# Deformable convolution band pipeline: offset bias carried by constant rows, f16 parts taken from PSUM, columns first in the offset convolution, one PSUM bank for turned windows and four for samples

## What is computed

```python
x = x + conv0(groupnorm(x))   # pair_repr @ Wa + ba, @ Wb + bb, sigmoid(@ Wg + bg),
                              # einsum('bijk,bikl->bijl', a, b), (g * ab) @ Wo + bo
x = x + conv1(groupnorm(x))   # deformable 3 x 3 convolution, below

def conv1(x, w_off, b_off, w_def):
    x = relu(x)
    offset = conv3x3(x, w_off) + b_off            # 18 values for each output pixel
    py = base_y + offset[:, :, 0]                 # 9 taps, each with a row and a column
    px = base_x + offset[:, :, 1]
    samp = bilinear_gather(x, py, px)             # 128 channels x 9 taps x pixels
    return einsum("bckhw,ock->bohw", samp, w_def)
```

## Time and profile before

| | before |
|---|---|
| median of 3 runs | 1659.01 us (1657.56 to 1660.0) |
| profiled execution, its own time | 1660.34 us |
| its span (first to last instruction) | 1658.2 us |
| PE busy | 1566.1 us, 94% |
| DVE busy | 1183.6 us, 71% |
| ACT busy | 1033.9 us, 62% |
| POOL busy | 919.9 us, 55% |

### The profile page before, as it was taken

How to read it: one execution, slowest core, us unless ns; L and a number is a source line. 1 busy time by engine, 2 the same in 40 slices (tenths; PEclk the granted TensorE clock), 3 DMA queues, 4 the chain that set the end, 5 groups by cost and what they waited for, 6 DMA issues and landing times.

```text
span 1658.2 us, 27065 instructions
## 1 busy us (share of the span) xinstructions
PE 1566.1 (94%) x8915; PEld 987.9 (60%) x8916; DVE 1183.6 (71%) x2218; ACT 1033.9 (62%) x1820; POOL 919.9 (55%) x555
## 2 busy tenths in 40 slices
PE   5999999948999999999999999999999999999998
PEld 3778787714555555555555555555555555555554
DVE  5888888745667777776777767777766777767764
ACT  2555555535666666666666666666666666666663
POOL 3555555616555555555555555555555555555561
PEclk9999999958999999999999999999999999999999
DMA  5333333245766666666666666666666666665550
GB/s 145 99 117 117 117 114 114 76 149 167 213 186 180 177 177 177 176 180 179 180 180 183 184 177 176 193 177 184 183 186 180 178 184 182 181 181 171 166 153 26
DMA packets 190601, 268.03 MB, mean 162 GB/s; under 512 B 19710, under 2 KB 128279, under 8 KB 190487
## 3 DMA queue, kind: packets, MB, share of 16 engines
q1 hardware_dynamic: 190486, 266.60, 55.0%
HBM read 188.33 MB, written 78.18 MB: 161 GB/s over the span
## 4 chain that ended last, share of the span: by engine, by line
PE 72%; issue 11%; POOL 6%; DVE 4%; SPq 3%; ACT 3%; DMA 1%; POOLq 0%; DVEq 0%; ACTq 0%
PE bank L827 29%; PE pair L796 22%; PE pair L873 9%; POOL samples_hi L1567 4%; PE pair L845 4%; PE bank L845 3%; DVE samples_lo L1359 2%; ACT samples_hi L1048 2%; PE pair L809 2%; PE pair L811 2%; POOL rstd L1542 1%; POOL samples_lo L1554 1%; SPq L490 0%; POOL weights L1619 0%; PE bank L704 0%
## 5 line engine op out<-in xcount | busy, mean ns | idle before, releaser
L1619 POOL TENSOR_TENSOR weights<-hy_all,hx_all 112x768 f32<-112x768 f32 x384 | 736.8, 1955 | 550.2 <-PE bank L827 507.0
L1359 DVE SCALAR_TENSOR_TENSOR samples_lo<-bank,samples_hi 128x288 f16<-128x288 f32 (+1 forms) x1024 | 450.7, 463 | 287.0 <-ACT samples_hi L1048 281.4
L827 PE MATMUL bank<-weights,zT 112*128 112x288 f32 (+1 forms) x2176 | 616.8, 408 | 24.2 <-DVE samples_lo L1359 24.0
L1048 ACT ACTIVATE samples_hi<-bank 128x288 f16<-128x288 f32 (+1 forms) x1024 | 413.6, 418 | 360.7 <-PE bank L827 330.3
L827 PEld LDWEIGHTS bank<-weights,zT 112*128 112x128 f32 x2176 | 374.5, 190 | 186.7 <-DVE samples_lo L1359 74.0
L796 PE MATMUL pair<-samples_hi,w_hi 128*128 128x512 f16 x576 | 218.8, 380 | 1.3 <-DVE samples_lo L1359 1.3
L796 PE MATMUL pair<-samples_lo,w_hi 128*128 128x512 f16 x576 | 217.5, 378 | 0.0
L796 PE MATMUL pair<-samples_hi,w_lo 128*128 128x512 f16 x576 | 217.4, 377 | 0.0
L1554 POOL TENSOR_TENSOR samples_lo<-samples_hi,samples_lo 128x512 f16<-128x512 f32 x64 | 74.2, 1159 | 130.1 <-ACT samples_lo L959 130.0
L950 ACT ACTIVATE samples_hi<-pair,nbias,rstd 128x512 f32<-128x512 f32 x64 | 49.8, 777 | 154.7 <-PE pair L695 97.5
L1336 DVE TENSOR_TENSOR offs_lo<-offs,offs_hi 114x512 f16<-114x512 f32 x64 | 135.3, 2113 | 2.2
(11 more groups left out here) (139 smaller groups left out, 1962.4 us busy)
## 6 DMA issues: line engine op xcount, KB each, us to landing
hy_all<-hat_y SPq DMA_DIRECT2D x384, 192.0 KB
hx_all<-hat_x SPq DMA_DIRECT2D x384, 192.0 KB
hat_y<-hats SPq DMA_DIRECT2D x256, 126.0 KB
raw<-x_pad SPq DMA_DIRECT2D x68, 272.0 KB, 4.4
x_pad<-hy_all SPq DMA_DIRECT2D x64, 272.0 KB, 3.3
weights<-in_x SPq DMA_DIRECT2D x64, 256.0 KB, 3.0
out<-y SPq DMA_DIRECT2D x32, 512.0 KB, 3.6
hat_x<-hats SPq DMA_DIRECT2D x128, 72.0 KB
```

Of the source, the lines that this page charges most:

```text
L827: mm = nc.tensor.matmul(sampled_step(n, p)[:, :, c0 - first:c1 - first], zT[0:WPIX, u * WINDOWS + w, :], weights[0:WPIX, u, :, c0:c1], sta ...
L1048: nc.scalar.activation(samples_hi[:, u, :, c0:c1], sampled_step(n, p), ACT.Copy).then_inc(samples_ready, 1)
L1359: nc.vector.scalar_tensor_tensor(out=samples_lo[:, u, :, c0:c1], in0=sampled_step(n, p), scalar=1.0, in1=samples_hi[:, u, :, c0:c1], op0=A ...
L1619: nc.gpsimd.tensor_tensor(to, hy_all[0:WPIX, i * TROWS:(i + 1) * TROWS, :], hx_all[0:WPIX, i * TROWS:(i + 1) * TROWS, :], ALU.mult).then_i ...
```

## The change

Five things are changed.

- **Bias.** The offsets' bias is no longer added by ACT. It becomes three rows of `select` (f16 parts of the bias, spread to the places that each offset has there), which meet three rows of ones in `offs_hi`. The parts are made once by POOL in groups 0 to 4 of the first block (`split_bias`), from a row loaded by SP.
- **Parts from PSUM.** ACT writes `offs_hi` (f16) straight from PSUM; DVE makes `offs_lo` in one instruction from PSUM and `offs_hi`. The f32 tile between them is gone.
- **Column order.** The offset convolution reads its pixels as 64 columns of 8 rows, instead of two halves of 64 columns of 4 rows, and writes PSUM in that order. The constant rows follow. `locate` now reads its f16 parts half by half: 64 runs of 4 values, twice.
- **Turns** all use bank 3; a turn waits for the copy of the one before.
- **Samples** rotate over four banks (4 to 7); a sample step waits for the `samples_lo` four steps back instead of three.

```diff
-SUM_ROWS = CONST_AT + 2 + RAMPS
+BIAS_AT = CONST_AT + 2 + RAMPS
+BIAS_PARTS = 3
+SUM_ROWS = BIAS_AT + BIAS_PARTS
...
-        B_OFF, B_CONV, B_ZT, B_S = 0, 2, (3, 4), (5, 6, 7)
+        B_OFF, B_CONV, B_ZT, B_S = 0, 2, 3, (4, 5, 6, 7)
...
+            for i in range(BIAS_PARTS):
+                sp.dma_start(ramps[BIAS_AT + i:BIAS_AT + i + 1, :],
+                             coords_d[0:1]).then_inc(in_select, 16)
...
+            sp.wait_ge(bias_set, 1)
+            sp.dma_start(bias_row[:, P + RAW_AT:P + CONST_AT],
+                         b_off.rearrange("(p a) -> p a", p=1)).then_inc(in_bias, 16)
...
+                if isinstance(g, int) and g == 7:
+                    sp.wait_ge(bias_set, BIAS_STEPS)
+                    for i in range(BIAS_PARTS):
+                        sp.dma_start(select[BIAS_AT + i:BIAS_AT + i + 1],
+                                     bias_parts[:, i].rearrange("p (a c) -> p a c", a=2)
+                                     ).then_inc(bias_placed, 16)
...
+                by_half = "p (w h r) -> p h w r"
                 for axis in range(2):
-                    nc.tensor.matmul(pairs[0][:, axis, :], select[:, axis, :],
-                                     offs_hi[:], start=True, stop=False)
-                    mm = nc.tensor.matmul(pairs[0][:, axis, :], select[0:CONST_AT, axis, :],
-                                          offs_lo[0:CONST_AT, :], start=False, stop=True)
+                    to = pairs[0][:, axis, :].rearrange("p (h w r) -> p h w r", h=2, r=HR)
+                    nc.tensor.matmul(to, select[:, axis, :],
+                                     offs_hi[:].rearrange(by_half, h=2, r=HR),
+                                     start=True, stop=False)
+                    mm = nc.tensor.matmul(to, select[0:CONST_AT, axis, :],
+                                          offs_lo[0:CONST_AT, :].rearrange(by_half, h=2, r=HR),
+                                          start=False, stop=True)
...
-                wait(pe, lows_ready, STEPS * n + p - 2)
+                wait(pe, lows_ready, STEPS * n + p + 1 - len(B_S))
...
-                elif g == 1:
-                    wait(pe, zT_v, zT_copied(n, 1)[1] - 1)
                 else:
-                    a, v = zT_copied(n, g - 2)
-                    pe.wait_ge(*((zT_a, a) if g % 2 == 0 else (zT_v, v)))
+                    a, v = zT_copied(n, g - 1)
+                    pe.wait_ge(*((zT_a, a) if g % 2 == 1 else (zT_v, v)))
...
-                        bank[B_OFF][at:at + width, :].rearrange("p (h w r) -> p h w r", h=2, r=HR),
-                        woff[:, k, 0:width],
-                        pixels[:, kx:kx + UW, ky:ky + BR].rearrange("p w (h r) -> p h w r", h=2),
+                        bank[B_OFF][at:at + width, :].rearrange("p (w r) -> p w r", r=BR),
+                        woff[:, k, 0:width], pixels[:, kx:kx + UW, ky:ky + BR],
...
-                wait(act, off_split, n)
-                nc.scalar.activation(offs4[0:CONST_AT, :], bank[B_OFF][0:CONST_AT, :], ACT.Identity,
-                                     bias=bias_off[0:CONST_AT, :],
-                                     scale=unscale[0:CONST_AT, OFF:OFF + 1]
-                                     ).then_inc(off_evicted, 1)
+                wait(act, located, n)
+                nc.scalar.activation(
+                    offs_hi[0:CONST_AT, :],
+                    bank[B_OFF][0:CONST_AT, :], ACT.Copy,
+                    scale=unscale[0:CONST_AT, OFF:OFF + 1]).then_inc(off_high, 1)
...
-                dve.wait_ge(off_evicted, n + 1)
+                dve.wait_ge(off_high, n + 1)
                 wait(dve, located, n)
-                nc.vector.tensor_copy(offs_hi[0:CONST_AT, :], offs4[0:CONST_AT, :]
-                                      ).then_inc(off_high, 1)
-                dve.wait_ge(off_high, n + 1)
-                nc.vector.tensor_tensor(offs_lo[0:CONST_AT, :], offs4[0:CONST_AT, :],
-                                        offs_hi[0:CONST_AT, :], ALU.subtract).then_inc(off_split, 1)
+                nc.vector.scalar_tensor_tensor(
+                    out=offs_lo[0:CONST_AT, :],
+                    in0=bank[B_OFF][0:CONST_AT, :],
+                    scalar=unscale[0:CONST_AT, OFF:OFF + 1],
+                    in1=offs_hi[0:CONST_AT, :],
+                    op0=ALU.mult, op1=ALU.subtract).then_inc(off_split, 1)
...
+            def split_bias(step):
...
+                if step == 0:
+                    pool.wait_ge(in_bias, 16)
...
+                pool.wait_ge(bias_set, step + 3)
+                left = bias_row if step < 2 else bias_rest
+                if step % 2 == 0:
+                    nc.gpsimd.tensor_copy(bias_parts[:, step // 2], left).then_inc(bias_set, 1)
+                else:
+                    nc.gpsimd.tensor_tensor(bias_rest, left, bias_parts[:, step // 2],
+                                            ALU.subtract).then_inc(bias_set, 1)
...
+                if isinstance(g, int) and g < 5:
+                    split_bias(g)
```

More of the change, by code:

```diff
@@ L67 @@
 IN_OFF = 16 * 3
-IN_SELECT, SELECT_STEPS = 16 * 29, 8
+IN_SELECT, SELECT_STEPS = 16 * (29 + BIAS_PARTS), 8
+BIAS_STEPS = 8
 BAND_STEPS, ROW_STEPS = 12, 2 + 4 * TAPS
@@ L211, in preact_conv_kernel @@
         z_hi, z_lo = (sb(n, [P, UW + 2, BR + 2], F16) for n in ("z_hi", "z_lo"))
-        offs4 = sb("offs4", [P, BW])
         offs_hi, offs_lo = (sb(n, [SUM_ROWS, BW], F16) for n in ("offs_hi", "offs_lo"))
@@ L236, in preact_conv_kernel @@
         y = sb("y", [P, 2, BR * WW])
+        bias_row, bias_rest = (y[0:1, 0, i * 2 * P:(i + 1) * 2 * P] for i in range(2))
+        bias_parts = (y[0:1, 1, :].bitcast(F16)[:, 0:BIAS_PARTS * 2 * P]
+                      .rearrange("p (i c) -> p i c", i=BIAS_PARTS))
         far_band = sb("far_band", [BANDS, 1])
@@ L262, in preact_conv_kernel @@
         in_select = sem("in_select")
+        in_bias = sem("in_bias")
+        bias_set = sem("bias_set")
+        bias_placed = sem("bias_placed")
         select_set = sem("select_set")
@@ L307, in preact_conv_kernel @@
         off_done = sem("off_done")
-        off_evicted = sem("off_evicted")
         off_high = sem("off_high")
@@ L406, in sampled_step @@
             first, end = step_columns(p)
-            return (bank[B_S[(STEPS * n + p) % 3]][:, 0:2 * TAPS * (end - first)]
+            return (bank[B_S[(STEPS * n + p) % len(B_S)]][:, 0:2 * TAPS * (end - first)]
                     .rearrange("p (k c) -> p k c", k=2 * TAPS))
@@ L490, in load_ramp @@
                     sp.dma_start(
-                        ramps[row:row + 1, :].rearrange("p (h w r) -> p h w r", h=2, r=HR)
+                        ramps[row:row + 1, :].rearrange("p (w h r) -> p h w r", h=2, r=HR)
                         [:, h, columns],
@@ L845, in turn_windows @@
                     mm = nc.tensor.transpose(
-                        bank[B_ZT[g % 2]][0:WPIX, (w % 4) * P:(w % 4 + 1) * P],
+                        bank[B_ZT][0:WPIX, (w % 4) * P:(w % 4 + 1) * P],
                         z[:, u, w].rearrange("p r c -> p (r c)"),
@@ L885, in _ @@
             pe.wait_ge(select_set, SELECT_STEPS)
+            pe.wait_ge(bias_placed, 16 * BIAS_PARTS)
             pe.wait_ge(scaling, W_STEPS)
@@ L1058, in copy_windows @@
                 nc.scalar.copy(zT[0:WPIX, at:at + c, :].rearrange("p w c -> p (w c)"),
-                               bank[B_ZT[0]][0:WPIX, 0:c * P]).then_inc(zT_a, 1)
+                               bank[B_ZT][0:WPIX, 0:c * P]).then_inc(zT_a, 1)
             act.wait_ge(select_set, SELECT_STEPS)
@@ L1210, in scale_weights @@
                     dve.wait_ge(in_select, IN_SELECT + 16)
-                    nc.vector.tensor_copy(select[:], chosen[0:SUM_ROWS])
+                    nc.vector.tensor_copy(select[0:BIAS_AT], chosen[0:BIAS_AT])
                     nc.vector.tensor_copy(offs_hi[RAW_AT:SUM_ROWS, :],
@@ L1379, in copy_windows @@
                 nc.vector.tensor_copy(zT[0:WPIX, at:at + c, :].rearrange("p w c -> p (w c)"),
-                                      bank[B_ZT[1]][0:WPIX, 0:c * P]).then_inc(zT_v, 1)
+                                      bank[B_ZT][0:WPIX, 0:c * P]).then_inc(zT_v, 1)
             def add_x1(n, u, k):
@@ L1536, in _ @@
             nc.gpsimd.memset(woff[:], 0.0)
+            nc.gpsimd.memset(bias_row, 0.0).then_inc(bias_set, 1)
             nc.gpsimd.memset(x1g, BELOW_ALL).then_inc(cleared, 1)
@@ L1557, in _ @@
             low_x(0)
+            def split_bias(step):
+                if step == 0:
+                    pool.wait_ge(in_bias, 16)
+                    of = bias_row[:, P + RAW_AT:P + CONST_AT]
+                    nc.gpsimd.tensor_copy(
+                        bias_row[:, 0:Y_ROWS].rearrange("p (g o k) -> p g o k", g=TROWS, k=TROWS),
+                        of.rearrange("p (g k d o) -> p g d o k", g=TROWS, k=TROWS, o=1)[:, :, 0]
+                        .broadcast_to([1, TROWS, SRC_R, TROWS])).then_inc(bias_set, 1)
+                    nc.gpsimd.tensor_copy(
```

(5 more changed lines are left out.)

## The result

The changed kernel takes 1605.9 us (median of 4 runs, 1603.74 to 1608.64) beside 1658.28 us (4 runs, 1656.14 to 1660.0) for the kernel before: ratio 0.9686, 95% interval 0.9664 to 0.9708. The forecast was 1613, in a range from 1597 to 1636. The profiled execution took 1607.68 us, with a span of 1605.9.

The account below looks back on a forecast made before the run. PE was taken to bound the kernel, busy 197.07 of 200 us. Per band -0.49 - 0.06 - 0.26 = -0.81 us, times 62 is -50, plus 4 at the start; from 1660.3 profiled to a median of 1613 us, range 1597 to 1636.

Parts of the forecast that it names:

- Parts from PSUM: DVE's cast and subtraction become one instruction; PE hardly waited for them before s9 and s10: -0.06 us a band.
- the touched-lines rival: Offsets and locate: touched lines limit fetching, so runs of 8 and aligned runs of 4 go at full rate; 1597 us, chance 0.13.
- Four sample banks: Before sample step s2: it needs only an older low part, so 0.49 of 0.56 us a band is saved.
- the stop read from starts as 0.56 us: PE's stop at s2, once a band: 0.46 us lost before it starts plus 0.10 us in its two passes.
- The +0.07 before c0: Charge a band because c0's first matmul still needs s15's low part, with signal and weight loading: 0.07 us.
- One bank for turns: Turns wait for the preceding turn's copy, but the sample steps between hide it (0.73 us of slack at T4): cost 0.
- Column order, offsets: Offset convolution's 18 matmuls, 8 rounds: the excess of 0.065 us a round vanishes with runs of 8, saving 0.52 us a band.
- I take the run length as the cause in both: Offsets and locate: run length sets the excess; -0.52 + 0.26 = -0.26 us a band.
- Column order, locate: Locate's four matmuls, now reading runs of 4, each pay up to 0.065 us: +0.26 us a band.
- The rival of the tiles: Offsets and locate: tiles cost the excess, not runs, so both keep their pace; 1629 us, chance 0.24.
- the stop at s2 moves to c0: Rival at a band's start: the chain grows or c0's restart is as dear, half of 0.49 lost; 1628 us, chance 0.12.
- The start: First block: POOL waits for the bias row's DMA, delaying early groups; +4 us once, bounds +1.5 and +10.

Follow-up runs that it names:

- the bank kernel: The kernel before with only the bank change, one bank for turns and four for samples: 1626.25 us, ratio 0.980.
- the later order: The changed kernel with offset convolution step O0 moved behind sample steps s5 and s6: 1592.42 us; the same order without parts from PSUM: 1599.64 us.
- halves again: The changed kernel with its offset convolution again reading and writing half by half, in runs of 4 f16: 1629.19 us, ratio 0.9817.
- the last kernel: The changed kernel with the bias row loaded early, O0 behind s5 and s6, and h0 behind s0: 1590.62 us, ratio 0.9588.

## Why the prediction was right, and where it was off

The direction and the size were right, by 7 us. Part of that is luck: -0.81 us a band was forecast and -1.02 came in undisturbed bands, of which an unforeseen wait and what goes with it gave back 0.15; the mean fell by 0.88. Over 62 bands 0.15 is 9 us: without it the time would have been about 1597 (an estimate from the pitches), the figure of the touched-lines rival and the lower end of the range. The undisturbed pitch of 18.89 also lies nearer to that rival's 18.8 than to the forecast's 19.1.

- **Four sample banks** (-0.49): the stop read from starts as 0.56 us went whole, so the size forecast was 0.07 too small; the bank kernel shows the term by itself (-0.62 a band). The +0.07 before c0 did not come: the gap there is unchanged.
- **Parts from PSUM** (-0.06): alone 0.05, beside four banks 0.08, in the later order 0.17. `offs_lo` takes 742 ns; the bound scaled from 432 columns, "at most 608 x 512/432 = 0.72 us", was just too low. Why the old one took 2.18 us, a collision with POOL, the prediction did not ask.
- **One bank for turns** (0): right, no wait on `zT` is listed for PE from 600 to 1500 us in any of these traces.
- **Column order, offsets** (-0.52): measured -0.43. The step "I take the run length as the cause in both" is what failed. That reading sets the cost is shown (halves again: +0.44); but it goes by lines touched, and taps 3 to 5 keep 0.05 us a matmul for a reason that stays open. "The same with two tiles and with four" held nearly (rounds of 281 to 288 and of 289 to 294 ns).
- **Column order, locate** (+0.26): measured +0.04. This was the largest error of a term. Runs of 4 at a pitch of 16 bytes touch as few lines as they can. The rival of touched lines, given 0.13, had this right; it expected the offsets at full rate, which they are not. The rival of the tiles is ruled out: on the same tiles the reading order moves the pitch by 0.44. The two errors of the column order go opposite ways, 0.09 too much and 0.22 too little saved, -0.39 in place of -0.26.
- **The sum.** It adds the parts as if each were worth the same whatever the others do. Alone, the banks, the column order and the parts from PSUM move the pitch by -0.62, 0 and -0.05, together by -1.02. The column order alone gave nothing: 0.43 saved on PE went into the wait before s10. Adding was nearly right here because four banks take that wait away: without the parts from PSUM 0.32 of the 0.39 is left, with them the rest.
- **Not foreseen:** the wait for `z_lo` in wrap bands, which with its after-effects costs 0.15 us a band in the mean. The prediction asked whether the stop at s2 moves to c0, but not what else it had given time to. `z_lo` was such a thing: 0.10 of the 0.15 come with the banks alone, the rest with the shorter `z_hi` part.
- **The start** (+4): measured +2.1. POOL did stop for 8.3 us, but until 33.73 and not about 36. The bias row's DMA was issued at 32.34, not 33.4: the three rows more on SP delayed nothing there. It released POOL 1.4 us later, not the 2.2 and more that I took from the earlier trace rows (and 33.4 + 0.4 + 2.2 is 36.0, not 35.8). The stop of the earlier trace rows paid back most of the rest.

## What to carry to other kernels

Before you book a saving on the engine that bounds a kernel, follow the next buffer it needs: where another engine's chain runs from the saved piece to that buffer, the saving turns into a wait until the chain is shortened or a buffer added. When a wait goes or an instruction gets shorter, list what it had given time to. When an instruction takes several times as long as the same one in a quiet stretch, look for what runs beside it before you make it shorter. Price an access pattern by the memory lines it touches, counted with pitch and start, not by the length of its runs.

## What the runs showed of the hardware

- At 2.4 GHz a matmul's moving operand in f16 cost about 1.78 ns for each move to another 16-byte line, where that exceeds the 0.213 us of 512 columns (230, 281 to 289, 334 to 346 ns at 128, 160, 192 moves); taps 3 to 5 in runs of 8, at 269, do not fit. At 1.2 GHz hardly anything of it shows (3.67 us beside 3.41 for the 18 matmuls).
- Matmuls on two column tiles side by side ran at full rate where the lines allow it (216 to 217 ns a round); the fastest rounds of four took 230. Going back to the full array costs extra: the first f32 matmul behind them starts the next after 0.347 us instead of 0.242.
- DVE's subtractions of two SBUF operands wait for a product of POOL that started first: `z_lo` took 0.85 us when it did not have to and up to 2.55 when it did (that in the last kernel), `offs_lo` 0.69 and 2.18. The cast to `offs_hi`, with one operand, took 0.43 and up to 2.10. With one of its operands in PSUM `offs_lo` took 0.74 to 0.75 beside such products.
